# Neighbour maximum of a two-layer graph network: eight fetched rows reduced by one strided instruction instead of three halvings

## What is computed

```python
def reference(x, adj, L1_gnn_W, L1_gnn_a):
    def neighbour_max(h, adj):                      # layer 0
        masked = jnp.where((adj != 0)[:, :, None], h[None, :, :], neg)
        return jnp.where(has_nbr[:, None], jnp.max(masked, axis=1), 0)
    def attention(h, adj, W, a):                    # layer 1
        hw = h @ W
        e = (hw @ a1)[:, None] + (hw @ a2)[None, :]
        e = jnp.where(adj > 0, leaky_relu(e, 0.2), NEG)
        return elu(softmax(e, axis=1) @ hw)
    h = jnp.maximum(layernorm(x), 0.0)
    x = x + neighbour_max(h, adj)
    h = jnp.maximum(layernorm(x), 0.0)
    return x + attention(h, adj, L1_gnn_W, L1_gnn_a)
```

## Time and profile before

| | us |
|---|---|
| median of 3 runs | 821.1 (820.5 to 821.99) |
| the profiled execution | 821.55 |
| its span | 819.7 |
| VectorE busy | 746.0 (91%) |
| TensorE busy (matmul) | 713.4 (87%) |
| ScalarE busy | 475.1 (58%) |
| GpSimd busy | 344.1 (42%) |

### The profile page before, as it was taken

The page is one execution under the profiler, slowest core; times in us unless marked ns, Lnnn a source line. Parts: engine busy times, 40 slices in busy tenths (PEclk is TensorE's granted clock), DMA queues, the critical chain, the costliest instruction groups (busy, mean ns, idle before and its releaser), DMA issues.

```text
span 819.7 us, 14960 instructions
## 1 busy us (share of the span) xinstructions
PE 713.4 (87%) x5658; PEld 507.7 (62%) x5658; DVE 746.0 (91%) x1248; ACT 475.1 (58%) x589; POOL 344.1 (42%) x322
## 2 busy tenths in 40 slices
PE   1788999899899899899898994576899999999995
PEld 1344555455455455455454553465899999999995
DVE  8999999999999999999999998944678998998894
ACT  2778899889899899899898881451320110010000
POOL 1511046556465565656656566374021330331230
PEclk9899999999999999999999997668999999999998
DMA  9799878998788888787887546023134434444410
GB/s 309 237 384 330 287 223 262 302 320 257 243 239 268 252 262 263 210 264 264 254 258 247 187 118 242 16 53 87 60 148 167 145 139 155 167 150 147 145 62 14
DMA packets 64904, 166.75 MB, mean 203 GB/s; under 512 B 7424, under 2 KB 12160, under 8 KB 60736
## 3 DMA queue, kind: packets, MB, share of 16 engines
q1 hardware_dynamic: 53776, 138.75, 48.3%
q0 software_dynamic: 11056, 27.02, 14.1%
HBM read 121.70 MB, written 44.04 MB: 202 GB/s over the span
## 4 chain that ended last, share of the span: by engine, by line
PE 38%; DVE 35%; issue 21%; POOL 3%; ACT 2%; DMA 1%; DVEq 0%; SPq 0%; POOLq 0%
DVE acc L774 14%; PE pick_ps L661 14%; PE order_ps L661 7%; DVE rest L763 5%; PE pick_ps L526 4%; PE key_ps L661 3%; PE flip_ps L661 3%; DVE second L760 3%; POOL found L313 3%; DVE tops L784 2%; DVE found L798 2%; DVE x L832 2%; PE flip_ps L500 1%; PE key_ps L539 1%; PE order_ps L509 1%
## 5 line engine op out<-in xcount | busy, mean ns | idle before, releaser
L313 POOL DMA_INDIRECT found<-subset_max,entry x256 | 270.3, 1056 | 216.4 <-DVE entry L788 131.5
L774 DVE TENSOR_TENSOR acc<-pick_ps,acc 128x1024 f32<-128x1024 f32 x240 | 284.4, 1219 | 2.4 <-PE pick_ps L526 2.3
L969 DVE SCALAR_TENSOR_TENSOR rest<-depth,acc,stage 128x512 f32<-128x512 f32 x256 | 201.4, 817 | 26.7 <-PE pick_ps L661 8.6
L349 ACT ACTIVATE first<-order_ps,neg 128x1024 f16<-128x1024 f32 x128 | 143.1, 1118 | 53.5 <-PE order_ps L509 53.2
L350 ACT ACTIVATE depth<-order_ps,mid 128x1024 f16<-128x1024 f32 x128 | 142.5, 1113 | 0.0
L341 ACT ACTIVATE edge_t<-flip_ps 128x1024 f16<-128x1024 uint16 x128 | 131.9, 1030 | 2.9 <-PE flip_ps L500 2.9
L661 PE MATMUL pick_ps<-keys,rest 128*128 128x129 f32 x1024 | 120.4, 279 | 12.0 <-DVE rest L969 12.0
L526 PE MATMUL pick_ps<-first,h_hi 128*128 128x512 f16 x256 | 97.7, 382 | 37.2 <-DVE acc L774 36.9
L661 PEld LDWEIGHTS pick_ps<-keys,rest 128*128 128x128 f32 x1024 | 118.7, 196 | 14.7 <-DVE rest L969 13.9
L500 PEld LDWEIGHTS flip_ps<-ident_h,stage 128*128 128x128 f16 x1024 | 67.8, 99 | 56.9 <-issue 17.0
L526 PE MATMUL pick_ps<-second,h_hi 128*128 128x512 f16 x256 | 97.7, 382 | 3.6 <-DVE second L760 3.4
(11 more groups left out here) (153 smaller groups left out, 809.1 us busy)
## 6 DMA issues: line engine op xcount, KB each, us to landing
stage<-adj SPq DMA_DIRECT2D x64, 1024.0 KB, 6.0
edge_units<-edge_t SPq DMA_DIRECT2D x64, 512.0 KB, 5.4
stage<-edge_units SPq DMA_DIRECT2D x32, 1024.0 KB, 4.8
subset_max<-keys POOLq DMA_DIRECT2D x12, 512.0 KB, 8.4
found<-subset_max,entry POOLq DMA_INDIRECT x256
best<-x SPq DMA_DIRECT2D x4, 512.0 KB, 6.2
subset_max<-x POOLq DMA_DIRECT2D x4, 512.0 KB, 6.3
out<-keys POOLq DMA_DIRECT2D x7, 256.0 KB, 2.8
```

The costliest lines, as they stand in the source:

```text
L313: nc.gpsimd.indirect_dma_start(found[:, n % NG, s, :], None, subset_max, bass.IndirectOffsetOnAxis(entry[:, n, s:s + 1], 0)).then_inc(gath ...
L349: nc.scalar.activation(first[:, g % 3, :], order_ps[:, :], ACT.Relu, scale=-1.0, bias=neg[:, :]).then_inc(first_ready, 1)
L774: V.tensor_tensor(acc[:, q % 2, k, :], pick_ps[k][:, :], acc[:, q % 2, k, :], ALU.max).then_inc(raised, 1)
L969: V.scalar_tensor_tensor(out=weight[:, n % WEIGHTS, :], in0=limit[:, q % 2, :], scalar=slope[:, c:c + 1], in1=units[:, m % EDGES, k * TI:( ...
```

## The change

`halve(n, 0)` now does the whole: one TENSOR_REDUCE over a view of the buffer in which the slot is the innermost dimension. It reads 1024 float32 values per partition, eight at a step of 512 bytes for each of the 128 results, and writes `left[:, n, :]`. `halve(n, 1)` and `halve(n, 2)` issue nothing. The calls stay where they were, and the semaphore `halved` is no longer used.

```diff
                 def halve(n, i):
-                    have = SLOTS >> i + 1
                     if i == 0:
                         dve.wait_ge(gathered[n % NG], 16 * SLOTS * (n // NG + 1))
-                    else:
-                        dve.wait_ge(halved, 2 * n + i)
-                    low, high = found[:, n % NG, 0:have, :], found[:, n % NG, have:2 * have, :]
-                    if have > 1:
-                        V.tensor_tensor(low, low, high, ALU.max).then_inc(halved, 1)
-                    else:
-                        V.tensor_tensor(left[:, n:n + 1, :], low, high, ALU.max).then_inc(reduced, 1)
+                        V.tensor_reduce(left[:, n, :], found[:, n % NG, :, :].rearrange("p s d -> p d s"), AX.X, ALU.max).then_inc(reduced, 1)
```

## The result

| | kernel before | changed kernel |
|---|---|---|
| median of 4 runs, us | 820.8 (820.3 to 822.0) | 845.4 (841.5 to 847.9) |
| ratio | | 1.0293 (95%: 1.0247 to 1.034) |
| the profiled execution, us | 821.55 | 841.5 |
| its span, us | 819.7 | 839.7 |
| VectorE busy, us | 746.0 | 767.8 |

The forecast was 850.0 in 820.3 to 853. The direction and the place of the loss were right; the price of a strided value was too high. So the two traces are compared with each other, and they are 20.0 us apart.

The account below looks back on a forecast made before the run. The prediction took VectorE to bound the main loop and TensorE the attention. The profiled 821.55 + 27.0 (main loop) + 1.8 (passage) gave 850.35 us, stated as 850.0 in a range of 820.3 to 853.

Parts of the forecast that it names:

- What bounds the kernel: VectorE bounds the main loop, TensorE the attention; VectorE changes count fully in the former, not at all in the latter.
- the main loop: 25 blocks whose VectorE distance per block rises from 1.12 to 2.20 us; 27.0 us added, all on the full engine.
- VectorE alone is full: In a main-loop tile VectorE is busy 58.97 of 59.00 us, TensorE 53.64, ScalarE 52.68.
- Rival (c): Reduce reads two values per clock, 693 ns; main loop -12.8 us, passage -1.4, kernel 807 us; chance 0.06.
- What is removed: Three halvings per block, 0.60, 0.33 and 0.19 us by distance, 1.12 us together; 1.38 us where they stand in a row.
- What is added: One strided reduce of 1024 values per block, taken as 2280 ns long with a distance of 2.20 us.
- the nearest whole price is a second clock: A strided value in the reduce was taken to cost two clocks of 1.04 ns instead of one.
- Rival (b): Reduce pays L881's excess, 0.63 to 0.84 ns per value; distance 1.79 to 2.00 us, kernel 838.9 to 844.5 us; chance 0.13.
- 512 bytes being no better than 32: The reduce's stride of 512 bytes should cost no less per value than the 32 bytes of L881.
- The cover of short steps: In the main loop TensorE's 0.6 us lag covers short steps; booked at nothing, up to 0.4 us per period if gone.
- The passage: Between main loop and attention, blocks 25 and 30 each lengthen the chain by 0.9 us; 1.8 us added.
- the two-clock case: Each strided value of the reduce takes two clocks; kernel 850.0 us, by itself 848 to 853; chance 0.50.

Follow-up runs that it names:

- last2: Kernel before with only the last of three halvings left in the main loop (six of eight fetched rows left out); 815.5 us, ratio 0.9915.
- contig2: Changed kernel with the reduce reading neighbouring columns, without the stride (wrong values), second run; 827.1 us, ratio 1.007.
- probe: Separate kernel of single VectorE instructions at various read steps; reduce of eight values per result 1221 ns in order, 1945 ns at a step of 4.
- probe2: Second separate kernel of single VectorE instructions, varying how many values make a result; two values 1230 ns, four values 1885 ns.
- Shift: Changed kernel with the reduce one step later, so the two short steps follow each other; 848.7 us, ratio 1.0312.
- loop2: Changed kernel with the strided reduce only in the main loop's 25 blocks, three halvings in the passage, second run; 843.0 us, ratio 1.025.
- again: Changed kernel unaltered, run once more on another chip; 842.8 us, ratio 1.0243.
- contig: Changed kernel with the reduce reading neighbouring columns (wrong values), first run, on a disturbed chip; 957.3 us, ratio 1.053.
- loop: Changed kernel with the strided reduce only in the main loop, halvings in the passage, first run, on a disturbed chip; 952.6 us, ratio 1.052.
- last: Kernel before with only the last halving left in the main loop, first run, on a disturbed chip; 932.8 us, ratio 1.031.
- even: Kernel before with all three halvings, the last one step later, on a disturbed chip; 847.2 us, ratio 0.948.

## Why the prediction came out as it did

**What bounds the kernel** was half right. VectorE is full in the main loop and additions count there in full: 25 x 0.72 = 18.0 us of the 19.8. But the step "VectorE alone is full" rested on busy times of 53.64 in 59 us for TensorE, and last2 showed that with the search and the last halving in one step TensorE allows no shorter period either. Rival (c), priced at -12.8 us in the main loop for a VectorE relieved of 0.5 us per block, was priced too high: a relief of 0.93 us brought 6 to 8 us in all.

**What is removed**: 1.12 us per block, right; contig2 replaced it by 1.13 (169.44 to 170.57), close to the 1.14 that the prediction gave to a reduce at the plain rate.

**What is added** is the term that was mis-sized: 2.28 us duration and 2.20 distance forecast, 1.91 and 1.84 measured. The step that failed was "the nearest whole price is a second clock", which no row asked for. The rows themselves gave 0.63 to 0.84 ns per value, and 1911 - 1215 = 696 ns over 1024 values is 0.68. Rival (b), which took the rows as they stand, gave 838.9 to 844.5 us; the profiled execution took 841.5, and the duration of 1.91 us and the period of 14.92 are those named for (b). The median of 845.4 lies above its range because three of the four runs had a lower mean clock, for which the prediction had no term. That this brought the median closer to 850.0 is luck: the trace that the forecast was made for stands at 841.5 against 850.35, of which the main loop has 7.2 us (27.0 forecast, 19.8 measured) and the passage 1.6. The rest of the argument, that L881 is the one strided reduce and shows the penalty although it is a single record of 32 values, was right, and the part on 512 bytes being no better than 32 as well (1872 and 1982 ns, L45 and L43 of probe). One thing it passed over: L881 reads SBUF, while the three rows that it is compared with read `key_ps`, which lies in PSUM. It did no harm, since 32 values in order from SBUF took 185 ns in probe2, where L1029 took 183.

**The cover of short steps** was booked at nothing, with up to 0.4 us per period if it failed. It held, but only just: 14.92 - 14.16 - 0.72 = 0.04 us per period, seen in the pair of maxima ahead of the search, which lasts 2.45 us in place of 2.35. Over the main loop 19.8 - 18.0 = 1.8 us are more than the reduces add: 0.2 us in each full tile, and 0.7 in the last one, where 0.45 us stand as a wait for `pick` (at 517.40). Shift shows what a failed cover costs: 0.45 us in each period without a `fold`.

**The passage** was booked at 1.8 us, which at the true rate is 1.0, and gave 0.24. First two rows of the kernel before, from VectorE's timeline and from the chain:

```profile
522.53 1.15 DVE L798 TENSOR_TENSOR found<-found 128x512 f32<-128x512 f32 x2
```

```profile
554.52 3.12 DMA found<-subset_max,entry
```

The chain of the changed kernel:

```profile
542.33 1.89 DVE left L793
544.26 0.70 issue
544.96 0.94 POOL found L313
...
574.36 2.89 DMA found<-subset_max,entry
577.32 1.75 issue
579.06 0.75 DVE rest L963
```

From the first `halve` to POOL's first fetch 2.63 us, before 2.22 (522.53 to 524.75); from the landing of block 30 to `weigh` 1.79 (577.27 to 579.06), before 1.39: both 0.4 us more, as the rate says. In between POOL's run is shorter, 574.36 - 544.96 = 29.40 us against 554.52 - 524.75 = 29.77, and so is the transfer behind it (2.89, before 3.12). POOL's fetches last 1023 ns in the mean where they lasted 1056. That VectorE's two-operand halvings slow them is an explanation that I didn't test by itself. The traces kept agree with it: the 26 fetches of this stretch last 984 ns in the mean in the kernel before, and 994 in loop2 and 991 in last2, which also halve here, but 970 in the changed kernel, 968 in shift and 950 in contig2.

**The chances**: the two-clock case had 0.50 and (b) 0.13; by the rows (b) should have had the larger share.

## What the runs showed of the hardware

**A strided write costs as much as a strided read** in a maximum of two tensors at a step of 16 bytes (1067 and 1058 ns, in order 693). I had expected it to be free.

**The granted clock.** The changed kernel's runs spread over 7 us, the kernel before's over 3.5, and both follow the mean granted clock of TensorE: 0.971 with 840.9 and 841.1 us, 0.960 with 844.5, 0.956 with 847.9 (the changed kernel on the chip of again); 0.972 with 820.05, 0.960 and 0.962 with 823.2 to 823.5 (the kernel before there). At an equal clock, 0.971, the two stand 21 us apart. In the trace of again (845.6 us span) the 6 us by which it is longer than the first trace of the changed kernel lie in three places; one of them, in stretches and in the timeline of VectorE:

```profile
215.00:222.00 7.00, 5.34 (x48) 3.10 (x46) 6.97 (x10) 6.45 (x8) 5.78 (x5) 1.00 0.79 234
222.00:234.00 12.00, 10.56 (x59) 5.18 (x59) 9.57 (x14) 6.11 (x8) 3.07 (x4) 0.72 0.49 154
```

```profile
228.62 1.23 DVE L774 TENSOR_TENSOR acc<-pick_ps,acc 128x1024 f32<-128x1024 f32 x1 [2.19 <-PE pick_ps L526]
```

At a granted 0.72, a mean between the levels of 1.2 and 2.4 GHz, TensorE becomes the bound for some microseconds, and the period that holds it is 19.26 us instead of 16.74. That the uneven steps bring the clock down more often (theory K) was not seen on an undisturbed chip: the mean over the runs was 0.965 for the kernel before, 0.965 for the changed one and 0.963 for contig2 beside it. On the disturbed chip it was 0.94 to 0.96 for the kernel before and 0.89 to 0.92 for contig, loop and last, which is in keeping with K but may as well be an effect of the disturbance.

**A disturbed main loop.** On two of five chips, in the main loop from the second tile on, periods of 17 to 21 us mostly replace those of about 14.2 us, with the reduce, the halvings or one halving alike, with the DMA share lower and VectorE and TensorE both at about 80% of the span. The kernel even was out of it after its second tile, the four others that were traced on these chips were not. No run tells its cause.

## What to carry to other kernels

Before a tree of elementwise maxima is replaced by one reduce, look at the step of the innermost reads: in the probes, from 16 bytes on and with four or more values for a result, a float32 cost 0.7 ns more than its 1.04, so that the penalty of 290 values eats the fixed parts that are saved (0.2 us here). And without any stride the reduce took 1.21 us for 1024 values, where a maximum of two tensors took 0.68 us for 512 pairs. Where a row of the trace shows the very effect, take its price as it stands, and don't round it to a mechanism. And an engine with no idle row is not proof that it alone is the bound: price what is added to it in full, but what is taken away only after asking how long the engine next to it needs for the same period, and keep short steps apart (two in a row cost 0.45 us per period here).
